# Attention 0's product with the values, computed with the probabilities stationary, and its units two half steps earlier

## The chip, the cores and the metric

The kernel is one program for one core of a Trainium2 chip. The metric is the device time of one execution in microseconds (us). Five engines work side by side, each through its own list in order, and meet by semaphores: TensorE (PE; PEld are its weight loads, which the profile shows apart), VectorE (DVE), ScalarE (ACT), GpSimd (POOL) and SyncE (SP), which here only issues DMAs.

## What is computed

Two decoder layers on x of 4 x 256 x 256 (four batches of 256 tokens of width 256), each a residual sum over attention, a gate out of a selective scan, and a feed-forward part. The change lies in layer 0, where two things run side by side, its attention and its scan. Cut to what matters:

```
q, k, v = rope + layernorm of x @ Wq.T, Wk.T, Wv.T     # 8 query heads, 2 key heads, width 32
scores  = q @ k.T / sqrt(32);  allowed: (j <= i) and (j > i - 64)
scores  = tanh(scores / 30) * 30
out     = softmax(scores) @ v ;  x = x + out @ Wo.T

state = state * exp(delta * A[n]) + delta * u * B[n]   # the scan, for n in 0..15
y     = sum over n of state * C[n]
```

## The kernel before

**The scan.** 32 half steps (g = 0 to 31) make up the scan of layer 0: 16 states for each of two halves of the tokens. Half step g takes ACT's two exponentials (`ssm_da`, L544, into `dA`), DVE's product with B (`ssm_dbu`, L909) and its scan (`ssm_scan`, L917), a product with C (POOL for g = 4 to 26, L391; DVE for the others, L924), and PE's `acc(g)`, L1324: eight transposes into two PSUM banks, where the states are summed. Half step 16 begins the second half of the tokens, and its `acc` has eight transposes more. Buffers hold four half steps, so DVE's product of half step g waits for `acc(g-3)`, and ACT's exponentials of g for the scan of g-4.

**The attention.** 16 units (u = 0 to 15), each two of the four query heads of one key head in one batch. A unit is:

- `s0(u)` on PE (L1420 to L1422): for each of the two heads a bf16 matmul that puts the mask into a bank, and two f32 matmuls of 32 rows, for the first 128 keys and the second 128. The scores come out with keys on the partitions.
- ACT: tanh (L624) and two exponentials (L630, L631) into `PT0[u % 2]`, probabilities not yet divided by their sum, [key, head, key block, query].
- `pv0(u)` on PE (L1434): `V0`, 33 columns (32 values and a column of ones that gives the sums), is the stationary operand, and 512 columns of `PT0` move, for each of two key blocks. The result is 33 x 512, by values.
- `pv0_copy(u)` on ACT (L618): from PSUM bank 2 into `O0`, which lies in `tabs`.
- `pv0_tr(u)` on PE (L1446): four transposes of `O0` into bank 3, so that queries are on the partitions.
- `at0(u)` on DVE (L1035, L1038): reciprocal of the sums, and the product with it into `H`.

A matmul of f32 stands in the trace as two weight loads and two matmul instructions; a transpose as one of each.

**The order is written out by hand.** `AT0_AT[u] = 12 + u` ties unit u to a half step: DVE does `at0(u)` right behind the scan of half step 12 + u, ACT has issued the exponentials up to 13 + u when it turns to unit u + 1, and PE does `acc` up to 10 + u behind `pv0(u)`. On PE the order in one pass of the loop is `s0(u+1)`, `pv0_tr(u-1)`, `pv0(u)`, `acc`. After unit 8 (`A_TR_UNIT`) the first half of the attention's output is transposed (`a_tr(0)`, L1454) and copied by ACT (L612) and DVE (L1045); PE waits for both copies before `pv0(9)`. Behind the units come the projection `o0` (L1484), the rest of the half steps, and the end of the layer.

The waits between the engines in a unit, which the change touches, are these:

```
pe.wait_ge(s["pv0_copied"], u + 1)      # pv0_tr(u): ACT's copy of unit u
pe.wait_ge(s["at0_ready"], u)           # pv0_tr(u): DVE has read bank 3
pe.wait_ge(s["pv0_copied"], u)          # pv0(u): ACT has read bank 2
dve.wait_ge(s["pv0_tr"], u + 1)         # at0(u)
```

Of the kernel before, what the change touches and what calls it, by code (L numbers as in the profile page):

```python
# [15 lines left out]
P = 128  # L16
B, S, HID = 4, 256, 256
# [5 lines left out]
H0, KV0, D0, WIN0 = 8, 2, 32, 64  # L23
# [63 lines left out]
def build(nc, io, out):  # L87
    ctx = ExitStack()
    with ctx:
# [43 lines left out]
        ident = sb("ident", [P, P])  # L133
# [3 lines left out]
        tabs = sb("tabs", [P, 6, 2, D1])  # L137
# [37 lines left out]
        PT0 = [WB[:, 1, 4 * S * i:4 * S * i + 4 * S].rearrange("p (r k q) -> p r k q", r=2, k=2) for i in range(2)]  # L175
        st0 = ar(30, 4 * NT * NQKV0 // D0).rearrange("p (i n) -> p i n", i=4)

        V0 = ar(20, NT * (2 * D0 + 1)).rearrange("p (t n) -> p t n", t=NT)
        rden0 = sb("rden0", [P, 4])
        O0 = tabs[0:D0 + 1, :, :, :].rearrange("p a b c -> p (a b c)")[:, 0:2 * S]  # L180
        aT0 = hT
        QK0, QKV0 = Q0[:, :, 0:NQK0], Q0.rearrange("p t (n d) -> p (t n) d", d=D0)
        nh0 = NT * NQKV0 // D0
# [46 lines left out]
        def router(*shape):  # L230
# [11 lines left out]
        ps = ctx.enter_context(nc.psum_tensor("ps", [P, 8, 512], F32))  # L242
# [10 lines left out]
        names = """act_chain dve_chain pool_chain init lw_ready conv_mm conv_tanh u_half u_ready xdbl_mm xdbl_copied bc_stored0 bc_stored1  # L253
            dtpre_mm sp_abs sp_max sp_exp sp_one sp_ln delta_ready du_ready skip_ready da_cols_zero da_ready dbu_ready scan_done c_ready acc_mm y_out
            ln_mv ln_rstd ln_h ln_tr_mm ln_tr_act ln_tr_dve qkv0_mm qkv0_copied rope0_cos rope0_sin rope0_add rope0_mean rope0_rot rope0_sq rope0_rs rope0_done v0_ready k4_ready tr0_mm tr0_copied
            s0_mm s0_tanh s0_exp pv0_mm pv0_copied pv0_tr at0_den at0_ready a_tr_mm a_tr_act a_tr_dve o0_mm x_new fsc_ready gate_tanh gate_h gate_mm gate_t nega_exp nega_ready pt0_fill
            f_mm f_tanh f_hid fd_mm wdn_ready w1_mean w1_centered tabs_ready job_mm job_sq job_rot job_sum job_rstd job_add job_rope
            job_tr_mm job_tr_copied v_mm v_copied s1_mm s1_max s1_exp s1_rc s1_norm pt1_mm pt1_copied pv1_mm at1_copied o1_mm
            r_bias r_mm r_exp r_tr r_sum r_gate gt_mm gt_copied gate_stored h_hi h_lo_dve h_lo_pool w_hi w_lo
# [1 line left out]
        s = {n: sem(n) for n in names}  # L261
# [201 lines left out]
        def _(act):  # L463
            sc = nc.scalar
# [130 lines left out]
            for g in range(KV0):  # L595
                c = H0 * D0 + D0 * g
                sc.copy(K40[:, :, g, :].rearrange("p t (r d) -> p t r d", d=D0),
                        Q0[:, :, c:c + D0].unsqueeze(2).broadcast_to([P, NT, 4, D0])).then_inc(s["k4_ready"], 1)
            for g in range(KV0):
                c = NQK0 + D0 * g  # L600
                sc.copy(V0[:, :, (D0 + 1) * g:(D0 + 1) * g + D0], Q0[:, :, c:c + D0]).then_inc(s["v0_ready"], 1)
            for i in range(8):
                act.wait_ge(s["tr0_mm"], i + 1)
                g, part, hf = i // 4, (i // 2) % 2, i % 2
# [5 lines left out]
            def a_tr_copy(hf):  # L610
                act.wait_ge(s["a_tr_mm"], 2 * hf + 1)
                sc.copy(aT0[:, 0, 512 * hf:512 * hf + 512], ps[:, 2, :]).then_inc(s["a_tr_act"], 1)  # L612

            def pv0_copy(u):
                act.wait_ge(s["pv0_mm"], u + 1)
                if u:
                    act.wait_ge(s["pv0_tr"], u)
                sc.copy(O0, ps[0:D0 + 1, 2, :]).then_inc(s["pv0_copied"], 1)  # L618

            for u in range(UNITS0):  # L620
                act.wait_ge(s["s0_mm"], u + 1)
                if u >= 2:
                    act.wait_ge(s["s0_exp"], 2 * (u - 1))
                sc.activation(TH0[u % 2], ps[:, 0:2, 0:W0 + P], ACT.Tanh, scale=SCORE0).then_inc(s["s0_tanh"], 1)  # L624
                act.wait_ge(s["s0_tanh"], u + 1)
                act.wait_ge(s["pt0_fill"], 5)
                if u >= 2:
                    act.wait_ge(s["pv0_mm"], u - 1)
                pt = PT0[u % 2]
                sc.activation(pt[:, :, 0, 0:W0], TH0[u % 2][:, :, 0:W0], ACT.Exp, scale=SOFTCAP).then_inc(s["s0_exp"], 1)  # L630
                sc.activation(pt[:, :, 1, P:S], TH0[u % 2][:, :, W0:W0 + P], ACT.Exp, scale=SOFTCAP).then_inc(s["s0_exp"], 1)  # L631
                if u:
                    pv0_copy(u - 1)
                    if u - 1 == A_TR_UNIT:
                        a_tr_copy(0)
                steps_to(AT0_AT[u] + 1)
            pv0_copy(UNITS0 - 1)
            steps_to(LAYER_STEPS - 1)
            a_tr_copy(1)

# [189 lines left out]
        def _(dve):  # L830
# [187 lines left out]
            for k in range(4):  # L1018
                ch.link(v.tensor_tensor(st0[:, 3, :], st0[:, 2, :], st0[:, 2, :], ALU.mult))
                ch.link(v.scalar_tensor_tensor(st0[:, 3, :], st0[:, 3, :], -0.5, st0[:, 1, :], ALU.mult, ALU.mult))  # L1020
                last = v.scalar_tensor_tensor(st0[:, 2, :], st0[:, 3, :], 1.5, st0[:, 2, :], ALU.add, ALU.mult)
# [6 lines left out]
            def at0(u):  # L1028

                b, g, rp = unit0(u)  # L1030
                dve.wait_ge(s["pv0_tr"], u + 1)
                if u:
                    dve.wait_ge(s["at0_ready"], u)
                o = ps[:, 3, 0:4 * (D0 + 1)].rearrange("p (h d) -> p h d", d=D0 + 1)
                v.reciprocal(rden0[:], o[:, :, D0 * (1 - g)]).then_inc(s["at0_den"], 1)  # L1035
                dve.wait_ge(s["at0_den"], u + 1)
                c = P * g + 2 * D0 * rp
                v.tensor_tensor(H[:, 2 * b:2 * b + 2, c:c + 2 * D0].rearrange("p t (r d) -> p t r d", d=D0),  # L1038
                                o[:, :, g:g + D0].rearrange("p (t r) d -> p t r d", t=2),
                                rden0[:].rearrange("p (t r) -> p t r", t=2).unsqueeze(3).broadcast_to([P, 2, 2, D0]),  # L1040
                                ALU.mult).then_inc(s["at0_ready"], 1)
# [247 lines left out]
            with dve.Fori(0, E // WRING, 1) as i:  # L1289
                for k in range(WRING):  # L1290
                    p = k % 2
# [12 lines left out]
        def _(pe):  # L1304
            mm, tr = nc.tensor.matmul, nc.tensor.transpose
# [76 lines left out]
            for t in range(NT):  # L1382
# [3 lines left out]
                for c in range(HC):  # L1386
                    last = mm(ps[:, 4 + t % 4, 0:NQKV0], hT[:, c, P * t:P * t + P], WQKV0[:, c, :], start=(c == 0), stop=(c == HC - 1))
# [7 lines left out]
            for i in range(8):  # L1395
                g, part, hf = i // 4, (i // 2) % 2, i % 2
                if i >= 4:
                    pe.wait_ge(s["tr0_copied"], i - 3)
                for t in range(4):
# [6 lines left out]
                    last = tr(ps[:, i % 4, P * t:P * t + P], src, ident[:])  # L1406
# [19 lines left out]
            def pv0(u):  # L1426

                b, g, rp = unit0(u)
                pe.wait_ge(s["s0_exp"], 2 * (u + 1))
                pe.wait_ge(s["v0_ready"], KV0)  # L1430
                if u:
                    pe.wait_ge(s["pv0_copied"], u)
                for kb_ in range(2):
                    last = mm(ps[0:D0 + 1, 2, :], V0[:, 2 * b + kb_, D0 * g:D0 * g + D0 + 1], PT0[u % 2][:, :, kb_, :],  # L1434
                              start=(kb_ == 0), stop=(kb_ == 1))
                last.then_inc(s["pv0_mm"], 1)

            def pv0_tr(u):

                pe.wait_ge(s["pv0_copied"], u + 1)  # L1440
                if u:
                    pe.wait_ge(s["at0_ready"], u)
                for t in range(2):
                    for r in range(2):
                        c = (2 * t + r) * (D0 + 1)
                        last = tr(ps[:, 3, c:c + D0 + 1], O0[:, S * r + P * t:S * r + P * t + P], ident[0:D0 + 1, 0:D0 + 1])  # L1446
                last.then_inc(s["pv0_tr"], 1)

            def a_tr(hf):

# [15 lines left out]
            for u in range(UNITS0):  # L1466
                if u + 1 < UNITS0:
                    s0(u + 1)
                if u:
                    pv0_tr(u - 1)  # L1470
                if u == A_TR_UNIT + 1:
                    a_tr(0)
                    pe.wait_ge(s["a_tr_act"], 1)
                    pe.wait_ge(s["a_tr_dve"], 1)
                pv0(u)
                acc_to(AT0_AT[u] - 2)
            pv0_tr(UNITS0 - 1)

            def o0(hf):
                pe.wait_ge(s["a_tr_act"], hf + 1)  # L1480
                pe.wait_ge(s["a_tr_dve"], hf + 1)
# [257 lines left out]


UNITS0 = 2 * B * KV0
AT0_AT = [12 + u for u in range(UNITS0)]
A_TR_UNIT = UNITS0 // 2


def unit0(u):

    return u // (2 * KV0), (u // 2) % KV0, u % 2
# [194 lines left out]
```

## Time and profile before

| | us |
|---|---|
| three runs | 970.36, 974.41, 974.85 |
| median | 974.41 |
| the profiled execution, as a run | 966.19 |
| its span in the profile | 964.4 |
| PE busy | 797.7 (83%) |
| DVE busy | 696.4 (72%) |
| ACT busy | 478.8 (50%) |
| POOL busy | 269.3 (28%) |
| mean granted TensorE clock, share of full speed | 0.931 |

The span is cut into stretches with different limits, so the shares above say little about one of them. The attention of layer 0 lies between about 111 and 221 us. The granted clock has two levels in this trace, 1.2 GHz (a share of 0.50) and 2.4 GHz (1.00), and a view of stretches gives it for each.

### The profile page before, as it was taken

The page shows a single profiled execution, that of the slowest core. Times are in us where ns is not written, and L with a number is a line of the kernel's source. Part 1 is how long each engine was busy: PE and PEld are TensorE (multiplying, and loading weights), DVE is VectorE, ACT ScalarE, POOL GpSimd, SP SyncE. Part 2 cuts the span into 40 slices and gives each one's busy share as a digit, 9 for nine tenths or more (in the row PEclk, how much of TensorE's full clock was granted, in tenths as well). Part 3 has the DMA queues.
Part 4 walks back from the last instruction along what each step waited for, and adds up shares of the span by engine and source line. Part 5 has one row for each costly group of instructions (what it writes and reads, how often), then busy time and mean ns, then how long its engine had stood idle before and what let it go on. Part 6 is the DMA issues. An engine that isn't in the chain of part 4 may idle for free.

```text
span 964.4 us, 11928 instructions
## 1 busy us (share of the span) xinstructions
PE 797.7 (83%) x3952; PEld 568.7 (59%) x3952; DVE 696.4 (72%) x1067; ACT 478.8 (50%) x990; POOL 269.3 (28%) x178
## 2 busy tenths in 40 slices
PE   6751679997699996789988879888883799999997
PEld 2331456555433563566666656655762579999996
DVE  4889677688976986999899788879937734444443
ACT  1743546561326302667657556656772444445442
POOL 1000344342231021111101111201003457666663
PEclk9785679899899999999999999999996899999999
DMA  4314132234220112011110111111200044334331
GB/s 163 119 39 139 66 109 96 80 110 153 98 93 0 66 44 88 23 45 55 33 63 26 44 45 44 44 45 44 68 1 0 1 158 161 133 131 153 140 130 44
DMA packets 24208, 74.60 MB, mean 77 GB/s; under 512 B 3120, under 2 KB 5696, under 8 KB 23776
## 3 DMA queue, kind: packets, MB, share of 16 engines
q1 hardware_dynamic: 23776, 71.51, 20.9%
q10 hardware_dynamic: 384, 2.49, 0.8%
q8 instruction: 25, 0.41, 0.2%
q14 instruction: 23, 0.19, 0.1%
HBM read 72.55 MB, written 1.44 MB: 77 GB/s over the span
## 4 chain that ended last, share of the span: by engine, by line
PE 52%; DVE 23%; ACT 11%; issue 10%; POOL 2%; DMA 0%; POOLq 0%; DVEq 0%; ACTq 0%; SPq 0%
PE ps L1559 6%; DVE hS L917 6%; PE ps L1673 6%; PE ps L1674 6%; PE ps L1675 6%; PE ps L1520 3%; PE ps L1324 3%; PE ps L1434 3%; PE ps L1539 2%; PE ps L1638 2%; ACT dA L544 2%; PE ps L1421 2%; PE ps L1626 2%; DVE hS L909 2%; DVE arena L1189 2%
## 5 line engine op out<-in xcount | busy, mean ns | idle before, releaser
L1324 PE MATMUL ps<-ident,hS 128*128 128x128 f32 x512 | 72.6, 291 | 49.2 <-DVE hS L924 26.4
L1295 DVE SCALAR_TENSOR_TENSOR arena<-ps,arena 128x1024 f32<-128x1024 f32 x32 | 39.2, 1225 | 101.5 <-ACT arena L783 93.1
L917 DVE TENSOR_TENSOR_SCAN hS<-dA,hS 128x1024 f32<-128x1024 f32 x41 | 93.6, 2282 | 23.5 <-ACT dA L544 23.1
L1324 PEld LDWEIGHTS ps<-ident,hS 128*128 128x128 f32 x512 | 62.0, 150 | 77.4 <-DVE hS L924 28.7
L1559 PE MATMUL ps<-WB,hT 128*128 128x512 f32 x192 | 90.7, 618 | 3.8 <-DVE arena L1170 2.0
L391 POOL TENSOR_TENSOR hS<-hS,BCb 128x1024 f32<-128x1024 f32 x23 | 56.1, 2440 | 131.5 <-DVE ps L909 115.3
L419 POOL TENSOR_SCALAR jst<-jst 128x8 f32<-128x8 f32 x20 | 12.3, 614 | 277.4 <-DVE jst L1178 277.4
L433 POOL TENSOR_TENSOR MHl<-arena,MHh 128x1024 fp32r<-128x1024 f32 x34 | 81.8, 2405 | 17.2 <-ACT MHh L786 17.2
L544 ACT ACTIVATE dA<-DEL,negA 128x510 f32<-128x510 f32 x128 | 84.7, 718 | 2.2 <-DVE hS L917 1.8
L1673 PE MATMUL ps<-Wh,MHh 128*128 128x256 f32 x272 | 78.2, 288 | 6.2 <-POOL MHl L433 6.2
L1675 PE MATMUL ps<-Wh,MHl 128*128 128x256 f32 x272 | 78.0, 287 | 0.0
L1674 PE MATMUL ps<-Wl,MHh 128*128 128x256 f32 x272 | 78.0, 287 | 0.0
L1638 PE MATMUL ps<-WA,arena 128*128 128x256 f32 x256 | 65.8, 380 | 2.4 <-DVE X L1227 2.4
L430 POOL TENSOR_TENSOR Wl<-WB,Wh 128x512 fp32r<-128x512 f32 x34 | 47.3, 1393 | 62.8 <-ACT Wh L767 62.8
L1559 PEld LDWEIGHTS ps<-WB,hT 128*128 128x128 f32 x192 | 37.9, 199 | 43.1 <-issue 42.1
L917 DVE TENSOR_TENSOR_SCAN hS<-dA,ps 128x1024 f32<-128x1024 f32 x23 | 52.6, 2287 | 8.8 <-ACT dA L544 8.0
L1673 PEld LDWEIGHTS ps<-Wh,MHh 128*128 128x128 f32 x272 | 53.1, 195 | 8.4 <-POOL MHl L433 7.3
L1617 PE MATMUL ps<-ident,arena 128*128 128x128 f32 x192 | 32.5, 278 | 29.5 <-ACT arena L736 25.4
L1674 PEld LDWEIGHTS ps<-Wl,MHh 128*128 128x128 f32 x272 | 53.2, 196 | 1.2
L1673 PE MATMUL ps<-hTh,Wh 128*128 128x512 f32 x136 | 53.6, 394 | 0.3 <-DVE arena L1295 0.3
L1674 PE MATMUL ps<-hTl,Wh 128*128 128x512 f32 x136 | 53.3, 392 | 0.0
L1675 PEld LDWEIGHTS ps<-Wh,MHl 128*128 128x128 f32 x272 | 53.2, 196 | 0.0
(223 smaller groups left out, 1941.3 us busy)
## 6 DMA issues: line engine op xcount, KB each, us to landing
BCb<-bc_dram SPq DMA_DIRECT2D x64, 512.0 KB, 3.6
arena<-gate_dram SPq DMA_DIRECT2D x32, 512.0 KB, 3.6
WB<-in_we SPq DMA_DIRECT2D x34, 256.0 KB, 2.7
WB<-in_wqkv SPq DMA_DIRECT2D x1, 3072.0 KB, 12.8
WA<-in_wo ACTq DMA_DIRECT2D x1, 2048.0 KB, 7.7
WA<-in_ffn SPq DMA_DIRECT2D x1, 1408.0 KB, 8.0
pkb<-in_pk SPq DMA_DIRECT2D x2, 698.0 KB, 4.6
X<-in_x SPq DMA_DIRECT2D x1, 1024.0 KB, 7.9
```

Of the source, the lines that this page charges most:

```text
L391: gp.tensor_tensor(h, h, BCb[g % SB_LOADS][:, 1:2, :].broadcast_to([P, DT, HALF]), ALU.mult).then_inc(s["c_ready"], 1)
L430: gp.tensor_tensor(Wl[:, slot, :], src, Wh[:, slot, :].bitcast(F32), ALU.subtract).then_inc(s["w_lo"], 1)
L433: gp.tensor_tensor(MHl[:, p, :], MH[p], MHh[:, p, :].bitcast(F32), ALU.subtract).then_inc(s["m_lo"], 1)
L544: sc.activation(bands2(ring(dA, g)[:, d, :]), bands2(DEL[:, d, pair(pr)]), ACT.Exp, scale=negA[:, d * DS + n:d * DS + n + 1]).then_inc(s[" ...
L917: v.tensor_tensor_scan(f(h), f(a), f(dbu(g)), 0.0, ALU.mult, ALU.add).then_inc(s["scan_done"], 1)
L1295: v.scalar_tensor_tensor(MG[p], f, 0.0, GB[k], ALU.max, ALU.mult).then_inc(s["m_gated"], 1)
L1324: last = mm(ps[:, ACC_BANK + j // 2, 256 * (j % 2) + P * d:256 * (j % 2) + P * d + P], src[:, d, P * j:P * j + P], ident[:], start=(first ...
L1559: last = mm(ps[:, bank + t, :], hT[:, c, P * (2 * b + t):P * (2 * b + t) + P], WB[:, c, c0:c0 + 512], start=(c == 0), stop=(c == HC - 1))
L1638: last = mm(ps[:, 5, 256 * t:256 * t + 256], aT1[u % 2][:, P * t:P * t + P], WO1[:, h, :], start=(h == 0 and t == 0), stop=(h == H1 - 1), ...
L1673: mm(out, wh, xh, start=start, stop=False, **kw)
L1674: mm(out, wh, xl, start=False, stop=False, **kw)
L1675: return mm(out, wl, xh, start=False, stop=stop, **kw)
```

## The change

The product with the values is turned round. The stationary operand is now a 128 x 128 block of the probabilities (one head, one block of keys, 128 queries), and the 33 columns of `V0` move. The result has queries on the partitions at once. There are eight such matmuls in a unit (two query blocks, two heads, two key blocks), the last two summed in PSUM, into bank 2 or 3 by turns. `pv0_copy`, `pv0_tr`, `O0` and their two semaphores go. DVE's `at0(u)` waits for `pv0_mm`, and `pv0(u)` for `at0(u-2)`. `AT0_AT` is `10 + u`, so each unit is tied to a half step two earlier.

```
-                if u:
-                    pv0_copy(u - 1)
-                    if u - 1 == A_TR_UNIT:
-                        a_tr_copy(0)
+                if u - 1 == A_TR_UNIT:
+                    a_tr_copy(0)
                 steps_to(AT0_AT[u] + 1)
-            pv0_copy(UNITS0 - 1)
...
-                dve.wait_ge(s["pv0_tr"], u + 1)
+                dve.wait_ge(s["pv0_mm"], u + 1)
...
-                o = ps[:, 3, 0:4 * (D0 + 1)].rearrange("p (h d) -> p h d", d=D0 + 1)
+                o = ps[:, 2 + u % 2, 0:4 * (D0 + 1)].rearrange("p (h d) -> p h d", d=D0 + 1)
...
-                if u:
-                    pe.wait_ge(s["pv0_copied"], u)
-                for kb_ in range(2):
-                    last = mm(ps[0:D0 + 1, 2, :], V0[:, 2 * b + kb_, D0 * g:D0 * g + D0 + 1], PT0[u % 2][:, :, kb_, :],
-                              start=(kb_ == 0), stop=(kb_ == 1))
-                last.then_inc(s["pv0_mm"], 1)
-
-            def pv0_tr(u):
-
-                pe.wait_ge(s["pv0_copied"], u + 1)
-                if u:
-                    pe.wait_ge(s["at0_ready"], u)
+                if u >= 2:
+                    pe.wait_ge(s["at0_ready"], u - 1)
                 for t in range(2):
                     for r in range(2):
                         c = (2 * t + r) * (D0 + 1)
-                        last = tr(ps[:, 3, c:c + D0 + 1], O0[:, S * r + P * t:S * r + P * t + P], ident[0:D0 + 1, 0:D0 + 1])
-                last.then_inc(s["pv0_tr"], 1)
+                        for kb_ in range(2):
+                            last = mm(ps[:, 2 + u % 2, c:c + D0 + 1], PT0[u % 2][:, r, kb_, P * t:P * t + P],
+                                      V0[:, 2 * b + kb_, D0 * g:D0 * g + D0 + 1], start=(t == 0 and r == 0 and kb_ == 0),
+                                      stop=(kb_ == 1), skip_group_check=True)
+                last.then_inc(s["pv0_mm"], 1)
...
-AT0_AT = [12 + u for u in range(UNITS0)]
+AT0_AT = [10 + u for u in range(UNITS0)]
```

How the change moves instructions on PE, from unit 0's product to unit 1's. Of before (L1434 is the product, L1324 the transposes of `acc`, L1420 to L1422 `s0`, L1446 the transposes of unit 0's result):

```order
24 L1434 MATMUL ps<-WB,arena 33x512 x2
25 L1324 MATMUL ps<-ident,hS 128x128 x40
26 L1420 MATMUL ps<-mask,identb 128x320
27 L1421 MATMUL ps<-arena 128x192
28 L1422 MATMUL ps<-arena 128x128
29 L1420 MATMUL ps<-mask,identb 128x320
30 L1421 MATMUL ps<-arena 128x192
31 L1422 MATMUL ps<-arena 128x128
32 L1446 MATMUL ps<-ident,tabs 128x33 x4
33 L1434 MATMUL ps<-WB,arena 33x512 x2
34 L1324 MATMUL ps<-ident,hS 128x128 x8
```

Of the changed kernel, at the same place (its L1427 is the product, L1314 `acc`, L1410 to L1412 `s0`):

```order
24 L1427 MATMUL ps<-arena,WB 128x33 x8
25 L1314 MATMUL ps<-ident,hS 128x128 x24
26 L1410 MATMUL ps<-mask,identb 128x320
27 L1411 MATMUL ps<-arena 128x192
28 L1412 MATMUL ps<-arena 128x128
29 L1410 MATMUL ps<-mask,identb 128x320
30 L1411 MATMUL ps<-arena 128x192
31 L1412 MATMUL ps<-arena 128x128
32 L1427 MATMUL ps<-arena,WB 128x33 x8
33 L1314 MATMUL ps<-ident,hS 128x128 x8
```

Behind unit 0's product stand three `acc` (half steps 6, 7 and 8) in place of five, the transposes are gone, and two matmuls of 512 columns are eight of 33.

On DVE, at the first unit. Of before (L909 the product with B, L917 the scan, L1035 and L1038 `at0`; the last scan ahead of `at0(0)` is that of half step 12):

```order
73 L909 TENSOR_TENSOR ps<-DU,BCb 128x1024
74 L917 SCALAR_TENSOR_TENSOR hS<-dA,ps 128x1024
75 L909 TENSOR_TENSOR ps<-DU,BCb 128x1024
76 L917 SCALAR_TENSOR_TENSOR hS<-dA,ps 128x1024
77 L1035 RECIPROCAL rden<-ps 128x4
78 L1038 TENSOR_TENSOR H<-ps,rden 128x2x64
79 L909 TENSOR_TENSOR ps<-DU,BCb 128x1024
```

Of the changed kernel (its L899, L907, L1025 and L1028):

```order
71 L899 TENSOR_TENSOR ps<-DU,BCb 128x1024
72 L907 SCALAR_TENSOR_TENSOR hS<-dA,ps 128x1024
73 L1025 RECIPROCAL rden<-ps 128x4
74 L1028 TENSOR_TENSOR H<-ps,rden 128x2x64
75 L899 TENSOR_TENSOR ps<-DU,BCb 128x1024
```

`at0(0)` stands four instructions, that is two half steps, earlier.

## Rows read from the trace of the kernel before

**Rows 1.** The page: its span, and the chain of waits by engine.

```profile
span 964.4 us, 11928 instructions
...
PE 52%; DVE 23%; ACT 11%; issue 10%; POOL 2%; DMA 0%; POOLq 0%; DVEq 0%; ACTq 0%; SPq 0%
```

**Rows 2.** Timeline of PE, one pass: start, us, engine, line, operation, what moved.

```profile
192.22 0.30 PE L1420 MATMUL ps<-mask,identb 128*128 128x320 bf16 x1
...
194.16 0.44 PE L1446 MATMUL ps<-ident,tabs 33*128 33x33 f32 x4
194.53 1.90 PE L1434 MATMUL ps<-WB,arena 128*33 128x512 f32 x4
196.37 1.09 PE L1324 MATMUL ps<-ident,hS 128*128 128x128 f32 x8
197.30 0.30 PE L1420 MATMUL ps<-mask,identb 128*128 128x320 bf16 x1
```

**Rows 3.** Timeline of DVE, one half step with its unit.

```profile
194.64 0.18 DVE L1035 RECIPROCAL rden<-ps 128x4 f32<-128x4 f32 x1 [1.11 <-PE ps L1446]
...
195.06 1.22 DVE L909 TENSOR_TENSOR ps<-DU,BCb 128x1024 f32<-128x1024 f32 x1
196.32 2.29 DVE L917 TENSOR_TENSOR_SCAN hS<-dA,ps 128x1024 f32<-128x1024 f32 x1
199.72 0.18 DVE L1035 RECIPROCAL rden<-ps 128x4 f32<-128x4 f32 x1 [1.11 <-PE ps L1446]
```

**Rows 4.** Timeline of DVE: the scans of half steps 12 and 26.

```profile
131.28 2.29 DVE L917 TENSOR_TENSOR_SCAN hS<-dA,ps 128x1024 f32<-128x1024 f32 x1
...
211.56 2.29 DVE L917 TENSOR_TENSOR_SCAN hS<-dA,ps 128x1024 f32<-128x1024 f32 x1
```

**Rows 5.** Timeline of the weight loads: stationary rows*columns, then what is loaded.

```profile
112.52 0.29 PEld L1421 LDWEIGHTS ps<-arena 32*128 32x128 f32 x2
...
132.18 0.50 PEld L1421 LDWEIGHTS ps<-arena 32*128 32x128 f32 x2 [0.46 <-issue]
...
189.08 0.32 PEld L1446 LDWEIGHTS ps<-ident,tabs 33*128 33x128 f32 x4
189.45 0.14 PEld L1434 LDWEIGHTS ps<-WB,arena 128*33 128x33 f32 x2
189.91 0.11 PEld L1434 LDWEIGHTS ps<-WB,arena 128*33 128x33 f32 x1 [0.32 <-issue]
...
286.37 0.18 PEld L1355 LDWEIGHTS ps<-dA,dtw 8*128 8x128 f32 x1 [0.24 <-issue]
```

**Rows 6.** Timeline of PE at half clock: an `acc`, then `s0`, then the transposes.

```profile
130.02 1.97 PE L1324 MATMUL ps<-ident,hS 128*128 128x128 f32 x8 [2.66 <-POOL hS L391]
131.78 0.47 PE L1420 MATMUL ps<-mask,identb 128*128 128x320 bf16 x1
...
135.29 0.63 PE L1446 MATMUL ps<-ident,tabs 33*128 33x33 f32 x4
```

**Rows 7.** Stretches: from:to, us, PE busy (matmuls), granted clock, DMA.

```profile
111.80:115.20 3.40, 2.52 (x15) 1.00 0.41 149
139.10:180.10 41.00, 40.40 (x217) 1.00 0.27 98
...
285.90:289.30 3.40, 3.40 (x8) 1.00 0.75 286
289.30:292.70 3.40, 3.40 (x5) 0.50 0.00 0
```

**Rows 8.** Timeline of PE: unit 0's product, and matmuls of eight rows.

```profile
116.90 3.62 PE L1434 MATMUL ps<-WB,arena 128*33 128x512 f32 x4
...
285.83 3.78 PE L1355 MATMUL ps<-dA,dtw 8*128 8x512 f32 x8
```

**Rows 9.** Timeline of PE: the transposes in the middle, and unit 9's product.

```profile
179.63 1.58 PE L1454 MATMUL ps<-ident,H 128*128 128x128 f32 x8 [0.60 <-DVE H L1038]
182.05 3.60 PE L1434 MATMUL ps<-WB,arena 128*33 128x512 f32 x4 [0.83 <-issue]
```

More of the change, by code:

```diff
@@ L179, in build @@
         rden0 = sb("rden0", [P, 4])
-        O0 = tabs[0:D0 + 1, :, :, :].rearrange("p a b c -> p (a b c)")[:, 0:2 * S]
         aT0 = hT
@@ L255, in build @@
             ln_mv ln_rstd ln_h ln_tr_mm ln_tr_act ln_tr_dve qkv0_mm qkv0_copied rope0_cos rope0_sin rope0_add rope0_mean rope0_rot rope0_sq rope0_rs rope0_done v0_ready k4_ready tr0_mm tr0_copied
-            s0_mm s0_tanh s0_exp pv0_mm pv0_copied pv0_tr at0_den at0_ready a_tr_mm a_tr_act a_tr_dve o0_mm x_new fsc_ready gate_tanh gate_h gate_mm gate_t nega_exp nega_ready pt0_fill
+            s0_mm s0_tanh s0_exp pv0_mm at0_den at0_ready a_tr_mm a_tr_act a_tr_dve o0_mm x_new fsc_ready gate_tanh gate_h gate_mm gate_t nega_exp nega_ready pt0_fill
             f_mm f_tanh f_hid fd_mm wdn_ready w1_mean w1_centered tabs_ready job_mm job_sq job_rot job_sum job_rstd job_add job_rope
@@ L612, in a_tr_copy @@
                 sc.copy(aT0[:, 0, 512 * hf:512 * hf + 512], ps[:, 2, :]).then_inc(s["a_tr_act"], 1)
-            def pv0_copy(u):
-                act.wait_ge(s["pv0_mm"], u + 1)
-                if u:
-                    act.wait_ge(s["pv0_tr"], u)
-                sc.copy(O0, ps[0:D0 + 1, 2, :]).then_inc(s["pv0_copied"], 1)
             for u in range(UNITS0):
@@ L1430, in pv0 @@
                 pe.wait_ge(s["v0_ready"], KV0)
-                if u:
-                    pe.wait_ge(s["pv0_copied"], u)
-                for kb_ in range(2):
-                    last = mm(ps[0:D0 + 1, 2, :], V0[:, 2 * b + kb_, D0 * g:D0 * g + D0 + 1], PT0[u % 2][:, :, kb_, :],
-                              start=(kb_ == 0), stop=(kb_ == 1))
-                last.then_inc(s["pv0_mm"], 1)
-            def pv0_tr(u):
-                pe.wait_ge(s["pv0_copied"], u + 1)
-                if u:
-                    pe.wait_ge(s["at0_ready"], u)
+                if u >= 2:
+                    pe.wait_ge(s["at0_ready"], u - 1)
                 for t in range(2):
@@ L1468, in _ @@
                     s0(u + 1)
-                if u:
-                    pv0_tr(u - 1)
                 if u == A_TR_UNIT + 1:
@@ L1476, in _ @@
                 acc_to(AT0_AT[u] - 2)
-            pv0_tr(UNITS0 - 1)
             def o0(hf):
```

## The prediction, made before the changed kernel was run

> **What bounds the kernel now.** I read the page first for the span and for the chain of waits by engine, where PE has 52% and DVE 23% [rows 1]; then the chain in order of time, to find the stretch of the change; then the timelines of PE and DVE there, because only they show which of the two waits for the other. In one pass of PE's loop nothing is idle: `s0` takes 1.94 us (192.22 to 194.16), the transposes of the last unit's result 0.37, the product 1.84, the `acc` 0.93, and the next pass begins 5.08 us after the last [rows 2]. DVE's half step has the same length, and 1.11 us of it is a wait for PE's transposes, so DVE alone would need 3.97 [rows 3]. PE is thus the bound of this stretch. The reader is to see a second thing, PE's clock: at half clock the same `s0` takes 3.51 us and an `acc` 1.76 [rows 6]. As a ruler I use the scans of half steps 12 and 26, whose order among the other work of DVE is the same in both kernels: they end at 133.57 and 213.85 [rows 4]. What follows half step 26 is the same work in the same order, apart from two `at0`, so a shift of that scan shifts the end.
>
> **What goes.** On PE the four transposes (0.37) and the old product (1.84) of each unit, 2.21 us on the path. On ACT a copy, which is off the path once PE no longer waits for it. On DVE nothing: `at0` has the same two instructions, and waits for the product itself. The queues behind that wait are as before: DVE's next product with B and its scan, and behind the scan POOL's product with C and an `acc` two half steps later. No DMA moves in the code; SP's loads follow the half steps.
>
> **What comes.** Eight f32 matmuls, so 16 weight loads of 128 columns and 16 instructions that move 33 columns. The old product moved 512 columns in 1.84/4 = 0.46 us, so 33 columns are 0.03 us. The load is dearer. Two loads of 128 columns of f32 together last 0.29 us and one 0.18, so one follows the other after 0.11; the same reckoning gives 0.03 for 33 columns (0.14 less 0.11) [rows 5]. In the transposes four loads of 128 columns last 0.32, and one is not over the 0.18 of the others, so they follow each other after at least 0.05 [rows 5]. The new loads are of ordinary matmuls of 128 columns, so the nearest row is 0.11, with the moving hidden behind the next load: 16 x 0.11 = 1.76 us. The upper end is load and moving in turn, 16 x 0.14 = 2.24; the lower end is the transposes' rate, 16 x 0.06 = 1.0. I take 1.76, because eight matmuls with loads of 128 columns took 3.78 us (0.47 each) [rows 8], while with loads of 33 columns they took 0.46 each [rows 2]: the larger load cost nothing there.
>
> The Trainium skill (TensorE: Matmul & The Clock Gate, What overlaps and what doesn't) says that a weight load overlaps a matmul in flight only if it is for another group of rows. By it the product would be the 2.24 us of the upper end, and the sum below 6 us more. The trace doesn't agree, by the two rows just named.
>
> **At full clock** a pass is then 1.94 + 1.76 + 0.93 = 4.63 us, above DVE's 3.97, so PE stays the bound and 0.45 us goes in each unit. The early start is worth more. Unit 0's product starts at 116.90 in both [rows 8]; behind it PE now needs only half steps up to 8 and goes on, where it used to stand still for the `acc` of 9 and 10 (one of these waits is 2.66 us [rows 6]). So when DVE has scanned half step 12, at about 134, the products of units 0 to 2 are there. From then: 13 passes for units 3 to 15, 60.2; the eight more transposes of half step 16, 0.9; the transposes in the middle and the copies behind them, 2.4 (179.63 to 182.05 [rows 9]); no `s0` in the last pass, -1.9; and from the last product over `at0` to the scan of half step 26, 4.0. That is 199.6 in place of 213.85, a gain of 14.2 us.
>
> **But the clock.** What decides is whether PE keeps its full clock. The new product keeps the array waiting for weights: 0.03 us of moving in each 0.11. In the trace the clock didn't ask whether PE had an instruction. From 285.90 to 289.30 PE was busy throughout, at a granted 1.00, with matmuls of only 8 of the 128 rows, and the clock fell to 0.50 in the next stretch [rows 7]. From 111.80 to 115.20 PE was busy for 2.52 of 3.40 us, most of it matmuls of 32 rows, and the next stretch was again at half clock, which is why unit 0's product took 3.62 us [rows 7, 8]. From 139.10 to 180.10 it was busy throughout too, and the clock held [rows 7]; there the old product moved columns through all 128 rows for 1.84 of every 5.08 us. The changed pass has left of such work 16 x 0.03 = 0.5 us in the product, an `acc` of 0.93, and `s0`, which is mostly matmuls of 32 rows. From the end of one `acc` to the start of the next it has 3.7 us of almost nothing but 32-row matmuls and weight loads. I read the rows as likening this more to 111.80 and 285.90 than to 139.10.
>
> The Trainium skill (TensorE: Matmul & The Clock Gate, What's actually happening) has it that the slow clock is the default and that a monitor of how busy PE has been gives the fast one. Taken as having instructions to run, by that rule the clock would hold, and the full-clock sum would be the result. The trace agrees as far as idle stretches go and speaks against that reading at 285.90.
>
> **At half clock** a pass is 3.51 for `s0`, 1.76 for the `acc`, and for the product twice the full-clock figure, 3.5 (two loads lasted 0.50 at half clock and 0.29 at full, a difference of 0.21 or 0.105 for each load [rows 5]): 8.77 us. Unit 0's product is then done at 120.4, and three `acc` in a row until about 125.5 are solid work of all rows and may bring the clock back for one unit. I put unit 2's product at 137.0. From there 13 passes of 8.77, 114.0; one of them at full clock behind the 16 transposes of half step 16, -4.1; these transposes 1.7; the middle 2.4; no last `s0`, -3.5; to the scan of half step 26, 4.0. That is 251.5 in place of 213.85: 37.7 us later. The copy of ACT that goes and the earlier start are worth nothing beside it.
>
> **Against the runs.** The profiled execution took 966.19 with a span of 964.4; it would become 1003.9. The median of the three runs is 974.41, 8 us above it, and I add the difference to that: 1012.
>
> **The rivals.**
>
> 1. The clock holds, since weight loads or the mere presence of matmuls count for it. For it: no gap is left in PE's list, and the stretch from 139.10 held its clock with over a third of the pass being 32-row matmuls. Against it: the two stretches above. Price: 974.4 - 14.2 = 960. This is the side opposite to my forecast, and it decides by one point, namely whether the stretch of `s0` and product is at 1.00.
> 2. The clock holds, and the load has another price. With load and moving in turn a pass is 5.1 us, and the gain 14.2 - 13 x 0.48 = 8: 966. With the transposes' rate DVE's 3.97 binds, the gain is 14.2 + 13 x 0.66 = 23: 951. Little speaks for the lower price, since the stationary operand isn't a transposed one.
> 3. A mixture: the clock falls and rises in turn. A unit at half clock costs 4.1 us more, so with four of sixteen at half clock the gain is used up, and with eight it is 15 to 20 us slower. For it: in the kernel before, the level is 1.00 at 111.80 and half again at 130.02 [rows 6, 7], though with gaps between.
> 4. Half clock and load and moving in turn: 13 x 0.96 = 12 us more than my forecast, 1024.
>
> **Chances.** Half clock for most of the units 0.52, of which case 4 is a small part; mixture 0.08, about evenly between gain and loss, with little in between; clock holds at my price 0.34, at the others 0.06. So faster by over 0.5% (about what a measurement of this kernel can tell from no change) 0.42; within 0.5% 0.04; slower 0.54. The forecast is the likeliest case, 1012, whose own range is 995 to 1024; the faster cases reach from 951 to 966. Both signs hold much of the chance, so the range must take in both: 948 to 1024.
>
> **What would show it.** The granted clock between 139 and 180 us: 0.50 for most of it if I am right, 1.00 if rival 1 is. The product's 16 matmuls: 1.76 us apart from first to the `acc` at full clock, 3.5 at half; 2.2 or 4.4 would be case 2 or 4. DVE's wait ahead of `at0`: some 4.8 us in each half step at half clock, 0.7 at full. `acc` 9 and 10 should no longer stand 2 us behind POOL. The scan of half step 26 should end at about 251, or at 200. What follows it should be as long as before; if it isn't, a step that I left out is at work. I am wrong if the clock holds, and then by the whole 52 us between the two sums.

## The result, and the profile after

The changed kernel takes 1001.91 us, the median of four runs (999.31 to 1004.84), and the kernel before 974.63 beside it (970.36 to 975.98): a ratio of 1.0288, with a 95% interval of 1.0238 to 1.0339. It is 27 us slower. The profiled execution of after took 1004.47. Each ratio, here and below, is of runs made beside each other, and isn't exactly the quotient of the two medians.

The page of after, against [rows 1]: the span, busy times, the clock in 40 slices, and the chain by engine.

```profile
span 1002.7 us, 12138 instructions
PE 843.4 (84%) x4080; PEld 637.7 (64%) x4080; DVE 696.3 (69%) x1067; ACT 469.5 (47%) x974; POOL 268.9 (27%) x178
...
PEclk9775655655878999899999999999998789999999
...
PE 56%; DVE 20%; ACT 10%; issue 10%; POOL 2%; DMA 0%; POOLq 0%; DVEq 0%; ACTq 0%; SPq 0%
```

PE is busy 46 us more (797.7 before), though it was given fewer columns to move. DVE's busy time is the same, and it waits more. The clock's slices from the fifth to the tenth say why. The same in stretches: from:to, us, busy time (and instructions) of PE and the others, then the granted clock.

```profile
126.10:129.50 3.40, 3.40 (x25) 2.88 (x23) 3.33 (x5) 1.41 (x3) 1.89 (x2) 1.00 0.40 153
129.50:194.30 64.80, 64.80 (x259) 56.36 (x258) 28.71 (x31) 20.41 (x37) 17.48 (x8) 0.50 0.19 65
194.30:204.60 10.30, 9.47 (x69) 8.05 (x68) 7.13 (x7) 6.12 (x12) 3.77 (x2) 1.00 0.16 51
204.60:248.90 44.30, 44.30 (x177) 39.02 (x177) 24.42 (x26) 16.17 (x29) 14.99 (x7) 0.50 0.22 72
```

For 64.8 us PE is never idle, and its clock is 0.50 throughout. The kernel before had 41.0 us at 1.00 in the same place [rows 7]. Over the whole span the level 0.50 lasts 250.6 us in after and 134.4 in before.

One pass of PE's loop in after, against [rows 2]: the product from 135.27, `acc`, the six rows of `s0`, and the next product.

```profile
135.27 3.62 PE L1427 MATMUL ps<-arena,WB 128*128 128x33 f32 x16
138.70 1.95 PE L1314 MATMUL ps<-ident,hS 128*128 128x128 f32 x8
140.44 0.47 PE L1410 MATMUL ps<-mask,identb 128*128 128x320 bf16 x1
...
143.95 3.62 PE L1427 MATMUL ps<-arena,WB 128*128 128x33 f32 x16
147.38 1.95 PE L1314 MATMUL ps<-ident,hS 128*128 128x128 f32 x8
...
198.16 1.95 PE L1427 MATMUL ps<-arena,WB 128*128 128x33 f32 x16 [0.83 <-ACT hT L611]
199.94 1.07 PE L1314 MATMUL ps<-ident,hS 128*128 128x128 f32 x8
```

A pass is 147.38 - 138.70 = 8.68 us: `acc` 1.74, `s0` 3.51, the product 3.43. The one at 198.16, at full clock, is followed by its `acc` after 1.78 us.

DVE in the same pass, against [rows 3], and the last scan of the ruler, against [rows 4].

```profile
147.61 0.18 DVE L1025 RECIPROCAL rden<-ps 128x4 f32<-128x4 f32 x1 [4.71 <-PE ps L1427]
...
246.28 2.29 DVE L907 TENSOR_TENSOR_SCAN hS<-dA,ps 128x1024 f32<-128x1024 f32 x1
```

DVE waits 4.71 us for the product where it waited 1.11 for the transposes. The scan of half step 26 ends at 248.57, 34.7 us later than before; the spans differ by 38.3.

### The profile page after: what moved, and what is told of

Same layout as the page of the kernel before. It is cut to its first block, busy times and chain, and to the rows that moved or that the text cites. A ratio compares the mean times of both kernels' runs of the same rounds, so it can differ in the third digit from the quotient of the medians.

```text
span 1002.7 us, 12138 instructions
## 1 busy us (share of the span) xinstructions
PE 843.4 (84%) x4080; PEld 637.7 (64%) x4080; DVE 696.3 (69%) x1067; ACT 469.5 (47%) x974; POOL 268.9 (27%) x178
## 4 chain that ended last, share of the span: by engine, by line
PE 56%; DVE 20%; ACT 10%; issue 10%; POOL 2%; DMA 0%; POOLq 0%; DVEq 0%; ACTq 0%; SPq 0%
PE ps L1538 6%; PE ps L1652 5%; PE ps L1653 5%; PE ps L1654 5%; PE ps L1427 5%; PE ps L1314 5%; DVE hS L907 5%; PE ps L1499 4%; PE ps L1411 3%; PE ps L1617 3%; PE ps L1518 2%; PE ps L1605 2%; ACT dA L543 2%; DVE hS L899 2%; DVE arena L1179 2%
## 5 line engine op out<-in xcount | busy, mean ns | idle before, releaser
L1314 PE MATMUL ps<-ident,hS 128*128 128x128 f32 x512 | 85.4, 326 | 45.5 <-DVE hS L914 26.1
L1314 PEld LDWEIGHTS ps<-ident,hS 128*128 128x128 f32 x512 | 75.7, 175 | 58.3 <-DVE hS L914 28.4
L907 DVE TENSOR_TENSOR_SCAN hS<-dA,hS 128x1024 f32<-128x1024 f32 x41 | 93.6, 2283 | 24.9 <-ACT dA L543 24.5
L1538 PE MATMUL ps<-WB,hT 128*128 128x512 f32 x192 | 87.9, 602 | 3.8 <-DVE arena L1160 2.0
L907 DVE TENSOR_TENSOR_SCAN hS<-dA,ps 128x1024 f32<-128x1024 f32 x23 | 52.6, 2287 | 8.8 <-ACT dA L543 8.1
L1427 PE MATMUL ps<-arena,WB 128*128 128x33 f32 x256 | 53.2, 381 | 0.8 <-ACT hT L611 0.8
L1427 PEld LDWEIGHTS ps<-arena,WB 128*128 128x128 f32 x256 | 51.3, 306 | 4.0 <-issue 2.7
```

Source lines behind the costliest of these rows:

```text
L907: v.tensor_tensor_scan(f(h), f(a), f(dbu(g)), 0.0, ALU.mult, ALU.add).then_inc(s["scan_done"], 1)
L1314: last = mm(ps[:, ACC_BANK + j // 2, 256 * (j % 2) + P * d:256 * (j % 2) + P * d + P], src[:, d, P * j:P * j + P], ident[:], start=(first ...
L1427: last = mm(ps[:, 2 + u % 2, c:c + D0 + 1], PT0[u % 2][:, r, kb_, P * t:P * t + P], V0[:, 2 * b + kb_, D0 * g:D0 * g + D0 + 1], start=(t = ...
L1538: last = mm(ps[:, bank + t, :], hT[:, c, P * (2 * b + t):P * (2 * b + t) + P], WB[:, c, c0:c0 + 512], start=(c == 0), stop=(c == HC - 1))
```

## The experiments

**Is it the number of columns that move?** The same product, at the same time, with 128 columns moving in each instruction rather than 33. What the 95 further columns give isn't read; each matmul's result begins at a multiple of 128 columns, and DVE's `at0` reads it there.

```diff
-                            last = mm(ps[:, 2 + u % 2, c:c + D0 + 1], PT0[u % 2][:, r, kb_, P * t:P * t + P],
-                                      V0[:, 2 * b + kb_, D0 * g:D0 * g + D0 + 1], ...
+                            v = 20 * kb + (2 * b + kb_) * (2 * D0 + 1) + D0 * g
+                            last = mm(ps[:, 2 + u % 2, c:c + 128], PT0[u % 2][:, r, kb_, P * t:P * t + P],
+                                      arena[:, v:v + 128], ...
```

> The changed kernel with 128 columns moving in each of the eight matmuls of a unit's product, in place of 33. The 95 columns more are whatever stands behind V0 in memory; their results are not read, and the output is the same. At half clock in the changed kernel one weight load follows the other 0.21 us after it, and 128 columns take as long, so the moving should be hidden behind the loads and the product take no longer. My theory (the clock fell because the array waits for weights in this product, with nothing moving through it): the clock is granted at 1.00 from about 139 to 180 us, a pass is 4.6 to 4.8 us, and the time is 960, the full-clock sum of the prediction (14 us under the kernel before, 42 under the changed one). Rival (the matmuls of 32 rows in s0, or the short pass, pull the clock down whatever the product moves): half clock stays, a pass of 8.7 us or a little more, about 1002.

Measured: 959.35 us (958.72 to 959.59), a ratio of 0.9871 (0.9808 to 0.9934) to 972.38 of the kernel before. Its stretches, and one pass of PE:

```profile
122.30:166.70 44.40, 43.57 (x317) 37.74 (x316) 36.05 (x39) 23.68 (x43) 21.62 (x10) 1.00 0.35 119
166.70:170.10 3.40, 3.40 (x17) 3.40 (x17) 3.14 (x2) 3.04 (x6) 2.37 (x1) 0.50 0.00 0
170.10:207.60 37.50, 32.84 (x237) 28.77 (x236) 30.93 (x31) 20.23 (x35) 20.83 (x8) 1.00 0.33 113
```

```profile
144.88 2.05 PE L1428 MATMUL ps<-arena,WB 128*128 128x128 f32 x16
146.76 1.04 PE L1314 MATMUL ps<-ident,hS 128*128 128x128 f32 x8
...
149.59 2.05 PE L1428 MATMUL ps<-arena,WB 128*128 128x128 f32 x16
```

Nearly four times the columns cost 0.1 us in a product (1.88 us from its first matmul to the `acc`, where the one of after at full clock had 1.78) and gave the clock back, but for one stretch of 3.4 us: 42.6 us less than after, from more columns moved. A pass is 4.71 us where the full-clock sum said 4.63. So the order of the work, the waits and the number of weight loads are not by themselves what made after slow.

**The two parts of the change apart.** The kernel before with only the early units (`AT0_AT` 12 to 10), then after with the late ones (`AT0_AT` back to 12), then the wide product with the late ones.

> The kernel before with the table of half steps alone changed, AT0_AT = 10 + u. The product, the copy and the transposes are the old ones. My theory: the full clock holds as before, the pass stays 5.08 us with PE as the bound. Unit 3's result comes at about the time at which unit 1's came (142 us), so the units run a little ahead of what they did, and half steps 26 and 27 come after the last unit, at DVE's own pace: 971, 2 to 4 us under the kernel before. Rival (the early start is worth much, since PE no longer waits for half steps 9 and 10): 6 to 10 us under it, 965 to 968. Rival (the early tie is what slows the changed kernel): over 990.

> The changed kernel with AT0_AT = 12 + u as before: the product alone is changed. My theory: half clock in most of the units, a pass of 8.7 us, so the last unit is done a few us later than in the changed kernel, but behind half step 27 and not 25, so that two half steps of DVE (some 8 us) no longer follow it: 997, about 5 us under the changed kernel. Rival (the early start is worth a gain at half clock too, or what comes after the units costs more): 1002 to 1010.

> The changed kernel with 128 columns moving in the product, as in the first of this call, and AT0_AT = 12 + u. The columns more are not read. My theory: full clock, a pass of 4.6 to 4.8 us; the last unit ends some 6 us later than with 10 + u, and two half steps (8 us) are behind it no more, so within 3 us of the first: 957 to 963. Rival (the early start is what brings the gain at full clock): 966 to 970.

Measured, beside 972.38 of the kernel before (the 1001.91 beside 974.63, as above):

| product | units from 12 on | units from 10 on |
|---|---|---|
| old, 512 columns | 972.38 | 966.69 (ratio 0.9943, 0.9914 to 0.9971) |
| new, 33 columns | 1011.93 (1.0419, 1.034 to 1.0498) | 1001.91 (1.0288, 1.0238 to 1.0339) |
| new, 128 columns | 964.05 (0.991, 0.9879 to 0.994) | 959.35 (0.9871, 0.9808 to 0.9934) |

The early units gain 5.7 us with the old product. I had expected 2 to 4, and 971; the rival's 965 to 968 was right. The scan of half step 26 ends at 209.01, 4.8 us earlier. Two stretches that before had at half clock, 128.9 to 139.1 and 180.1 to 186.9, are gone. At the first, PE's waits for POOL in the `acc` behind unit 0's product went from 2.21 and 2.66 us to one of 0.93. That these waits made the clock fall there is likely but not shown, and for the second stretch no cause is known.

```profile
121.10:213.30 92.20, 85.88 (x458) 52.05 (x456) 73.06 (x71) 58.20 (x105) 45.37 (x19) 1.00 0.30 103
```

The new product alone costs 40 us and not 25. I had expected stretches at full clock between, as after has one. The profile of that kernel (late units, 33 columns) has almost none:

```profile
129.00:187.00 58.00, 56.91 (x224) 49.33 (x225) 31.61 (x31) 17.54 (x31) 19.80 (x9) 0.50 0.22 74
187.00:190.40 3.40, 3.40 (x28) 3.01 (x27) 0.18 (x1) 2.06 (x5) 0.00 (x0) 1.00 0.48 154
190.40:262.10 71.70, 70.87 (x283) 61.73 (x282) 34.08 (x37) 24.25 (x44) 20.77 (x8) 0.50 0.18 58
```

Its last `at0` starts at 260.8 where after's starts at 244.6. By the medians the early units were worth 10.0 us at half clock (1011.93 less 1001.91); by the two profiled executions 4.3 (1008.80 less 1004.47), and in these the scan of half step 26 ends at 248.71 and 248.57, so the whole of it lies behind that scan. The rival's 1002 to 1010 was nearer than my 997 in either.

**Columns, or rows?** The wide product, with 128 columns moving, but with weights and moving columns in 32 rows only. It leaves out 96 of the 128 keys of each block, so its output is not the attention's.

```diff
-                            last = mm(..., PT0[u % 2][:, r, kb_, P * t:P * t + P], arena[:, v:v + 128], ...)
+                            last = mm(..., PT0[u % 2][0:32, r, kb_, P * t:P * t + P], arena[0:32, v:v + 128], ...)
```

> The version with 128 columns moving, but with 32 of the 128 rows only: keys 32 to 127 of each block are left out of the product, so attention 0 is computed from part of its keys. Number and order of instructions, columns loaded and columns moved are as in that version. My theory (what counts for the clock is what passes through all rows; matmuls of 8 rows lost it at 285.90 in the kernel before): half clock over most of the units, a pass of 8.7 us, 1000 to 1010. Rival (a column that moves counts whatever its rows): full clock, 959.

Measured: 979.53 (979.22 to 979.82), a ratio of 1.0077 (1.0045 to 1.011) to 973.74. That is between the two expectations, so the stretches decide:

```profile
121.60:138.70 17.10, 17.10 (x142) 14.37 (x140) 16.62 (x18) 9.92 (x19) 9.89 (x5) 1.00 0.37 126
138.70:172.80 34.10, 34.10 (x154) 29.14 (x153) 18.47 (x20) 12.44 (x23) 11.72 (x5) 0.50 0.26 92
172.80:183.00 10.20, 9.37 (x72) 7.87 (x71) 7.08 (x7) 5.89 (x11) 3.73 (x2) 1.00 0.14 53
183.00:224.00 41.00, 41.00 (x177) 34.98 (x175) 25.51 (x27) 17.46 (x31) 15.12 (x8) 0.50 0.23 79
```

The clock fell with 128 columns through 32 rows and, but for 3.4 us, held with 128 columns through 128. So it isn't the number of columns alone that held the clock in the wide product: without the other 96 rows they didn't. It fell later than in after (138.7 against 129.5), and the pass was shorter, for a reason that neither theory had. PE's timeline, two passes at full clock:

```profile
124.30 0.42 PE L1411 MATMUL ps<-arena 32*128 32x192 f32 x1
124.31 0.48 PE L1428 MATMUL ps<-arena,WB 32*128 32x128 f32 x2
124.56 0.32 PE L1411 MATMUL ps<-arena 32*128 32x192 f32 x1
...
124.86 1.50 PE L1428 MATMUL ps<-arena,WB 32*128 32x128 f32 x12
126.29 1.09 PE L1314 MATMUL ps<-ident,hS 128*128 128x128 f32 x8
...
130.42 1.09 PE L1314 MATMUL ps<-ident,hS 128*128 128x128 f32 x8
```

Product matmuls of 32 rows start while `s0`'s second half is still running, so `acc` follows `acc` after 4.13 us and not 4.7. This kernel differs from the wide one in more than the clock, and its time is no clean measure of the clock's part. The stretches are.

**Is it the long piece without work of all rows?** Each `acc` of units 1 to 7 and 9 to 15 has its eight transposes set one by one between the eight matmuls of a product that still moves 33 columns. The work of a pass is the same as in after. The piece without moving through all rows is shorter.

```diff
-                pv0(u)
-                acc_to(AT0_AT[u] - 2)
+                if u and u != A_TR_UNIT:
+                    pv0(u, next(step))
...
+                            if g_acc is not None:
+                                x = mm(ps[:, ACC_BANK + j // 2, ...], src[:, d, P * j:P * j + P], ident[:], is_transpose=True, ...)
```

> The changed kernel with 33 columns moving, as it is, and the eight transposes of an acc set between the eight matmuls of the product, one behind each, in units 1 to 7 and 9 to 15. The work of a pass is the same, in another order. A transpose moves 128 columns of all rows while the product's next weights are loaded, so the two parts hide each other: at full clock eight times (0.107 + 0.107 + 0.053 us of loads) = 2.1 us for both, in place of 1.76 + 0.93. My theory (the clock fell because product and s0 lie side by side as one long piece in which nearly nothing moves through all rows): the clock holds at 1.00 from 139 to 180 us, a pass is 4.1 us, close to DVE's own 3.97, and the time is 953, about 20 us under the kernel before. Rival (it is the sum of what moves in a pass that is too little, however it lies): half clock, a pass of 7.8 us, 996 to 1000.

Measured: 1004.92, 955.16, 1005.17 and 985.37 us, median 995.14. I give no ratio, because these four are not one time with noise. One run came within some 2 us of what I expected (953), two lay 5 us above the rival's 996 to 1000, and one lay between. The mean granted clock of the runs was 0.869, 0.920, 0.871 and 0.889. The profile is of the first:

```profile
129.90:246.00 116.10, 115.27 (x498) 99.09 (x497) 58.22 (x62) 42.47 (x76) 34.10 (x16) 0.50 0.20 67
```

The same instructions in the same order gave mean clocks as far apart as these, and in this execution, once at 0.50, the clock stayed there for 116 us. So the spacing alone held the clock in at most one run of four. To see whether columns do more, the next one has 80 of them in the same arrangement.

> The kernel with the transposes of acc between the product's matmuls, with 80 columns moving in each of these in place of 33 (the 47 more are not read). One group of two loads and moves of the product and one transpose needs 0.27 us for its loads and 2 x 0.067 + 0.107 = 0.24 us for what moves, so the pass should stay at 4.1 us at full clock. My theory (the runs of that kernel lie apart, 955 to 1005 us, because so little moves in a pass that the clock falls in some runs and, once at half, does not come back): with more moving every run holds the clock, 950 to 954, and the runs lie within 5 us. Rival (the order of short pieces, or something else of this version, loses the clock): the runs lie apart as before, up to 1005.

Measured: runs of 952.30, 953.99 and 955.98, a ratio of 0.9803 (0.9753 to 0.9852) to 970.50, and a fourth run of 1346.55 us, which the ratio leaves out. The mean granted clock of the fourth was 0.552, against 0.923 to 0.927 in the three, so that execution was at half clock nearly from end to end and not in the attention alone. It wasn't profiled, and nothing on record says whether the program or something else brought it about. My expectation that every run holds the clock is therefore not met. In the profiled execution (955.98) the clock held from 121.9 to 200.4:

```profile
121.90:200.40 78.50, 73.54 (x566) 63.60 (x564) 69.80 (x70) 45.70 (x82) 42.98 (x19) 1.00 0.36 121
...
146.34 0.18 DVE L1025 RECIPROCAL rden<-ps 128x4 f32<-128x4 f32 x1 [0.42 <-PE ps L1431]
...
150.73 0.18 DVE L1025 RECIPROCAL rden<-ps 128x4 f32<-128x4 f32 x1 [0.42 <-PE ps L1431]
```

A pass is 4.39 us against 4.71 of the wide product with its `acc` behind it. I had expected 4.1 and 950 to 954, so the pass was 0.3 us longer than I put it, and the three times lie about the upper edge.

**A better version.** With the clock held, what stands in the way is that DVE waits in every half step while later half steps have no unit. So on the wide product the units are spread: half steps 16 and 22 get none, and the last unit is tied to 27 in place of 25.

```diff
-AT0_AT = [10 + u for u in range(UNITS0)]
+AT0_AT = [10, 11, 12, 13, 14, 15, 17, 18, 19, 20, 21, 23, 24, 25, 26, 27]
```

> The version with 128 columns moving in the product (the 95 more are not read), and the units tied to half steps 10 to 15, 17 to 21 and 23 to 27: the first starts as early as in that version, the last is where it was in the kernel before. My theory: PE is the bound at 4.7 us a pass and DVE has 0.7 us to spare in each, so DVE can do two half steps more beside the units than behind them; the last unit ends within 2 us of that version's, and two half steps (3.75 us each) are no longer behind it: 952 to 954, against 959.35. Rival (what ends late is PE, or the half steps of POOL and the transposes behind the units hold the end where it is): 958 to 961.

Measured: 952.01 (947.61 to 953.91), a ratio of 0.9801 (0.9764 to 0.9838) to 973.74. It is the lowest median, as expected, though its runs overlap those of the 80 columns between the transposes (952.30 to 955.98). The last scan of the ruler ends at 195.32, where the wide kernel without the spread has it at 201.59:

```profile
193.03 2.29 DVE L907 TENSOR_TENSOR_SCAN hS<-dA,ps 128x1024 f32<-128x1024 f32 x1
```

Then the same table on the old product, to see whether the new product is needed for it:

> The kernel before, with its own product, copy and transposes, and the units tied to half steps 10 to 15, 17 to 21 and 23 to 27. My theory: this table is worth the same with either product as long as the clock holds: PE is the bound at 5.08 us a pass, DVE has 1.1 us to spare in each and does two half steps more beside the units, so 7 us less than the kernel before with the table 10 + u (966.7): 959 to 961. Rival (the table only pays together with the new product): 966 or more.

Measured: a ratio of 0.9936 (0.9899 to 0.9972) to 970.50, from nine runs of 962.08 to 970.32 with a median of 964.09. A tenth run took 4358.06 us, at a granted clock of 1.00, and isn't explained. The median lies between my 959 to 961 and the rival's 966 or more, and the ratio can't be told from that of the early units alone (0.9943). The nine fall into two groups, 962.08 to 964.09 and 968.64 to 970.32, and the profile is of the second: there the scan of half step 26 ends at 208.93, against 209.01 with the early units alone, so no gain is seen. PE of the old product at a half step without a unit, at the middle, and at the other half step without a unit:

```profile
154.90 1.09 PE L1324 MATMUL ps<-ident,hS 128*128 128x128 f32 x8
157.38 1.09 PE L1324 MATMUL ps<-ident,hS 128*128 128x128 f32 x8 [1.38 <-POOL hS L391]
...
175.12 3.59 PE L1434 MATMUL ps<-WB,arena 128*33 128x512 f32 x4 [0.83 <-issue]
...
191.45 1.09 PE L1324 MATMUL ps<-ident,hS 128*128 128x128 f32 x8 [1.37 <-POOL hS L391]
```

and PE and DVE of the wide one, at the first of these places:

```profile
152.99 1.91 PE L1314 MATMUL ps<-ident,hS 128*128 128x128 f32 x16
...
164.35 0.18 DVE L1025 RECIPROCAL rden<-ps 128x4 f32<-128x4 f32 x1 [0.42 <-PE ps L1428]
```

With the old product PE stood still for POOL's product with C at both half steps without a unit (1.38 and 1.37 us), which with the early units alone it does nowhere behind unit 0's `acc`, and its product in the middle ran at half clock (3.59 us, against 1.88 there). With the wide one PE doesn't wait at these half steps. I put this down to the place where a result is handed over: the old product's is ready only after the transposes in the next pass, behind two `acc`, the new one's in its own pass, ahead of them, so that DVE and POOL are further on. No run tests that.

## Why the prediction was right, and where it was off

**The side and the cause.** The forecast was that the clock falls, 1012 with 995 to 1024; the time is 1001.91. The whole range that I gave, 948 to 1024, was wide enough for either outcome, and slower had a chance of 0.54, so what counts for the argument is the clock and the terms, not that the time lies in the range. The clock between 139 and 180 us was to be 0.50 and is. The wide product, which changes little but the columns, shows that the loss goes with the clock: where it holds, the time is 959.35, and the first rival's price was 960. That rival's mechanism, that weight loads or the mere presence of matmuls keep the clock, is refuted by the 64.8 us in which PE was never idle. By the reading of the Trainium skill (TensorE: Matmul & The Clock Gate, What's actually happening) that the prediction weighed, "busy" as having instructions to run, the clock would have held. The trace disagrees, with the 0.50 of that stretch.

**The terms at half clock.** A pass 8.77, measured 8.68; the product 3.5, measured 3.43; unit 0's product done at 120.4, measured 120.78; DVE's wait 4.8, measured 4.71. Unit 2's product at 137.0, measured 138.93 by its `at0`; behind three `acc` the clock was at 1.00 for one unit, as forecast, for 3.4 us. At full clock the product was to be 1.76 and is 1.78. So 128 columns of weights follow each other after 0.11 us, and the 33 columns that move are hidden behind them. The lower end (1.0) and load and moving in turn (2.24, the second and fourth rivals) are both wrong. For the latter stood the Trainium skill (TensorE: Matmul & The Clock Gate, What overlaps and what doesn't), by which a load overlaps a matmul in flight only for another group of rows. The trace disagrees: the sixteen loads and their matmuls, all of the same rows, took 1.78 us.

**Between.** One unit at full clock behind the transposes of half step 16 was forecast; the level 1.00 lasted from 194.3 to 204.6, over the middle transposes and the products of units 9 and 10, whose `at0` came 3.9 us apart (201.4 and 205.3) and not 8.7. That is why the scan of half step 26 ended at 248.57 and not 251.5. The two errors, 1.9 later at unit 2 and earlier by the longer stretch, partly cancel.

**Behind the ruler** the work was to be as long as before. It is 754.1 us (1002.7 less 248.57) against 750.5 (964.4 less 213.85), 3.6 more. The clock is at half for a few stretches more there, such as 279.7 to 289.9 us. In the other kernels of this study the rest varies in the same way: from the scan of half step 36, in layer 1, on it is 619.2 us in before (964.4 less 345.2), 620.7 in after, and between 619.0 and 624.5 in the others. The two shortest, 619.2 and 619.0, are those of before and of the spread wide kernel, whose profiled executions (966.19 and 947.61) are also below their medians. The step that failed is the assumption of a fixed rest; the error is small.

**The term that was mis-sized** is the last one, from profile to median. The difference of the profiled executions was forecast as 37.7 and is 38.3. That these agree so well is partly luck: the scan of half step 26 came 2.9 us earlier than forecast and the rest took 3.6 us longer. I added it to the median, 974.41. But the profiled execution of before was at 966.19, below all four timed runs, and that of after, 1004.47, is in the upper pair of its four. The medians differ by 27.3. Had I added the 37.7 to the profiled time alone, I would have said 1003.9, 2 us off. The kernel's own spread (965 to 977 over 19 runs) is of the size of that error, and a median of three beside a single profile doesn't allow to add one to the other.

**"The earlier start is worth nothing beside it"** was wrong. At half clock it is worth 10.0 us by the medians and 4.3 by the profiled executions, with the old product 5.7, with the wide one 4.7 (964.05 less 959.35). The full-clock sum was right as a whole (960) and not in its parts: of its 14.2 it gave 13 x 0.45 = 5.9 to the shorter pass and 8.3 to the early start, and the runs of the wide product gave 8.3 to the product alone (972.38 less 964.05) and 4.7 to the start behind it.

**What stays open.** In the profiled executions the clock was lost with 33 columns in the product, held with 128, held with 80 set between the transposes, and lost with 128 through 32 rows. Eighty columns with the `acc` behind the product weren't run. The runs don't say whether weight loads count for something, since no run took loads away with the moving kept. Why the level 1.00 lasted 10.3 us in the middle of after and 3.4 in the kernel with late units isn't settled either. Nor is what puts one execution of the interleaved product at full clock and another at half; only an execution at half clock was profiled. The run of 1346.55 us is open too.

## What to carry to other kernels

When an edit swaps wide moving operands for weight loads and short ones, check the granted clock of the stretch before believing a sum of durations: PE can be busy for all of 64.8 us and yet be at half speed. If it falls, moving columns that nobody reads is a remedy worth a run; here 128 in place of 33 cost 0.1 us in a product and returned 42.6 us. Take several runs of it, since one of four with 80 columns took 1346.55 us. And ask of a cheaper instruction sequence what it does to the order as well: the spread units gained 6 to 7 us on the wide product (7.3 by the medians of two sets of runs, 6.3 by the scan of half step 26), and on the old one nothing that could be told from the early units alone.

## What the runs showed of the chip that was not expected

- The granted clock can have two courses for one program: the interleaved product with 33 columns took 955.16 us once, 1005 twice and 985.37 once, at a mean clock of 0.920, 0.87 and 0.889.
- One execution in four of the kernel with 80 columns took 1346.55 us at a mean granted clock of 0.552; the others took 952.30 to 955.98. Its cause is open.
- Wasted moving was nearly free here beside weight loads of 128 f32 columns: 1.88 us for a product with 128 columns moving, 1.78 with 33.
- Matmuls of 32 rows of the product and of `s0`, next to each other in PE's list, overlapped in the trace (124.30 and 124.31), and a pass became 0.6 us shorter at the full clock.
